# A 12-stage decoder kernel: masks of the turned scores moved from TensorE products to GpSimd selects, and another order at the end of a block step

## The reference

```python
# "block layer" (L1_attn): causal attention in windows of 128 that see the window before, norms and feed-forward
Q, K, V = (x @ proj + bias).reshape(B * 16, 256, 16)
sim = einsum('bnwd,bnkd->bnwk', qw * 16 ** -0.5, bk)       # keys: own and previous window
sim = where(key_position <= query_position, sim, -1e9)
attn = softmax(sim) @ bv
x = layernorm(x + attn, ln1_g, ln1_b)
ff = maximum(x @ ff1_w + ff1_b, 0.0) @ ff2_w + ff2_b
x = layernorm(x + ff, ln2_g, ln2_b)

# "cross-attention layer" (L1_xattn): a causal attention, then one over a context of 77 tokens
h = mha(x, x, x, causal=True)                              # 16 heads of 16
out = mha(h, encoder, encoder, causal=False)
```

## Time and profile before

| what | us |
|---|---|
| median of three runs | 3149.42 (3141.65 to 3149.58) |
| the profiled execution: span from first to last instruction | 3146.4 |
| its own time | not recorded apart from the span |
| TensorE, VectorE, ScalarE, GpSimd busy | 2939.7, 1864.8, 1253.5, 435.9 |
| block layer, 1137 to 1408: TensorE, VectorE, GpSimd busy | 242.29, 191.00, 21.48 |
| cross-attention layer, 1408 to 1688: TensorE, VectorE, GpSimd busy | 257.13, 191.32, 10.45 |

### The profile page before, as it was taken

The page is one execution under the profiler, slowest core; times in us unless marked ns, Lnnn a source line. Parts: engine busy times, 40 slices in busy tenths (PEclk is TensorE's granted clock), DMA queues, the critical chain, the costliest instruction groups (busy, mean ns, idle before and its releaser), DMA issues.

```text
span 3146.4 us, 52294 instructions
## 1 busy us (share of the span) xinstructions
PE 2939.7 (93%) x20677; PEld 1953.5 (62%) x20677; DVE 1864.8 (59%) x6449; ACT 1253.5 (40%) x1946; POOL 435.9 (14%) x458
## 2 busy tenths in 40 slices
PE   7999999998989889988998999899999999998998
PEld 4666666875555556655665566566666766766653
DVE  5534433599999636775777898574244344434455
ACT  2222221335656433323444678544323333323443
POOL 0010010114433221000000356300000000000000
PEclk9999999988999999999999899899999999998999
DMA  3000000010000100000000111100000000000000
GB/s 130 1 1 0 1 1 1 1 53 1 2 1 2 34 32 1 1 1 6 1 2 1 25 39 28 41 2 27 1 1 0 1 0 1 1 1 9 2 1 27
DMA packets 22028, 37.75 MB, mean 12 GB/s; under 512 B 2132, under 2 KB 19733, under 8 KB 20760
## 3 DMA queue, kind: packets, MB, share of 16 engines
q1 hardware_dynamic: 20968, 34.02, 3.2%
q10 hardware_dynamic: 816, 0.39, 0.1%
HBM read 26.81 MB, written 2.10 MB: 9 GB/s over the span
## 4 chain that ended last, share of the span: by engine, by line
PE 76%; DVE 17%; ACT 4%; issue 2%; DMA 0%; ACTq 0%; DVEq 0%; SPq 0%; POOL 0%; POOLq 0%
PE ps L416 44%; DVE arena L569 3%; PE ps L621 2%; PE ps L689 2%; PE ps L3098 2%; PE ps L3117 2%; ACT arena L675 2%; PE ps L1633 2%; PE ps L517 2%; PE ps L2353 2%; PE ps L2399 2%; DVE arena L1967 2%; PE ps L730 2%; PE ps L711 1%; PE ps L2971 1%
## 5 line engine op out<-in xcount | busy, mean ns | idle before, releaser
L416 PE MATMUL ps<-weights,arena 128*128 128x256 f32 (+4 forms) x2480 | 694.3, 429 | 41.3 <-DVE arena L1848 22.5
L416 PEld LDWEIGHTS ps<-weights,arena 128*128 128x128 f32 (+1 forms) x2480 | 459.5, 195 | 210.8 <-issue 92.9
L416 PE MATMUL ps<-arena,weights 128*128 128x256 f32 (+4 forms) x1726 | 558.9, 472 | 14.0 <-DMA weights<-in_w_L_attn 6.1
L416 PEld LDWEIGHTS ps<-arena,weights 128*128 128x128 f32 (+1 forms) x1726 | 315.1, 191 | 217.0 <-issue 156.5
L416 PE MATMUL ps<-arena 128*128 128x256 f32 (+4 forms) x1618 | 425.8, 416 | 6.8 <-ACT arena L4816 1.5
L416 PEld LDWEIGHTS ps<-arena 128*128 128x128 f32 (+2 forms) x1618 | 297.9, 188 | 115.4 <-issue 74.3
L569 DVE TENSOR_REDUCE arena<-ps 128x16 f32<-128x1232 f32 (+2 forms) x96 | 179.1, 1866 | 151.0 <-PE ps L547 51.8
L675 ACT ACTIVATE arena<-ps 77x2048 f32<-77x2048 f32 (+1 forms) x112 | 210.0, 1875 | 123.9 <-PE ps L621 61.8
L1967 DVE MATCH_REPLACE8 arena<-arena 128x77 f32<-128x77 f32 x1024 | 214.7, 228 | 0.0
L864 POOL TENSOR_TENSOR x<-x,weights 128x512 f32<-128x512 f32 x32 | 43.8, 1370 | 1194.9 <-DVE arena L830 1147.2
L2366 ACT ACTIVATE arena<-ps 128x1536 f32<-128x1536 f32 x128 | 185.5, 1451 | 51.4 <-PE ps L2355 44.6
(11 more groups left out here) (430 smaller groups left out, 4437.6 us busy)
## 6 DMA issues: line engine op xcount, KB each, us to landing
arena<-arena SPq DMA_DIRECT2D x156, 32.0 KB
weights<-in_w_L_ffn SPq DMA_DIRECT2D x1, 3848.0 KB, 11.5
weights<-in_w_L_attn SPq DMA_DIRECT2D x1, 3840.0 KB, 15.1
weights<-in_w_L_xattn SPq DMA_DIRECT2D x3, 1024.0 KB, 6.3
weights<-in_w_L_ffn SPq DMA_DIRECT2D x1, 3072.0 KB, 10.2
x<-in_x SPq DMA_DIRECT2D x2, 1024.0 KB
weights<-in_w_L_xattn SPq DMA_DIRECT2D x1, 2048.0 KB, 7.4
out<-x SPq DMA_DIRECT2D x8, 256.0 KB, 2.2
```

The costliest lines, as they stand in the source:

```text
L416: ins = k.nc.tensor.matmul(out, lhsT, rhs, start=start and i == 0, stop=i == n - 1)
```

## The change

Three edits, all for the causal batches of the two layers.

First, the "keyC" mask products of the turned scores go. Their job is done after the exponential, by GpSimd: `affine_select` keeps a probability where query >= key and writes 0.0 elsewhere. `hide_second_gpsimd` does `prob1` (four instructions of 128x4x128 behind `prob` 1), `hide_first_gpsimd` the first half of each 256 queries in `prob` (two behind `prob` 2, two behind `prob` 3); each signals `hidden`, and `pair_outputs_tensor` waits for `hidden` 2 + c. In round 0 two of the four places are now multiplied ahead of the turn of the maxima. Second, in the block layer the feed-forward's down product ("ff2") stands ahead of the next query, and the outputs of c = 0 come last; ScalarE's query copy stands ahead of `pair_raw_scalar` accordingly. Third, GpSimd's list is put in another order: its sum for x1 of batch n - 1 comes behind the selects of batch n, and in the cross-attention layer the bias sum of batch n + 1 comes behind the selects of batch n.

```diff
@@ turned_first_tensor
     after(pe, s, u, "top", u.a.rounds)
-    causal, places = u.a.causal, turned_places(u, 0)
-    if causal:
-        for i in range(4):
-            hide_later(k, k.ps[:, HI + i, :], mask_of(k, "keyC"))
-    else:
-        turned_products(k, s, u, places[0], True, False)
+    places = turned_places(u, 0)
+    ahead = 2 if u.a.causal else 1
+    for n, place in enumerate(places[:ahead]):
+        turned_products(k, s, u, place, n == 0, False)
     turn_tops_tensor(k, pe, s, u, b, at)
-    for place in places if causal else places[1:]:
+    for place in places[ahead:]:
         turned_products(k, s, u, place, False, False)
@@ turned_scores_tensor
     after(pe, s, u, "prob", r)
-    if u.a.causal:
-        for i in range(4):
-            hide_later(k, cut(k.ps[:, HI + i, :], slot=4)[:, 0::2, :], mask_of(k, "keyC")[:, 0:2 * P])
     for place in turned_places(u, r):
-        turned_maxima(k, s, u, place, not u.a.causal, False)
+        turned_maxima(k, s, u, place, True, False)
@@ pair_outputs_tensor
     if u.a.causal:
         after(pe, s, u, "kv")
+        after(pe, s, u, "hidden", 2 + c)
@@ new
+def hide_second_gpsimd(k, pool, s, u):
+
+    after(pool, s, u, "prob", 1)
+    for j in range(4):
+        prob = s.prob1[:, :, j * P:(j + 1) * P]
+        ins = k.nc.gpsimd.affine_select(prob, prob, [[0, 4], [1, P]], ALU.is_ge, 0.0, base=0, channel_multiplier=-1)
+    ins.then_inc(*s.sig.up(u.a.p + "hidden"))
+
+
+def hide_first_gpsimd(k, pool, s, u, c):
+
+    after(pool, s, u, "prob", 2 + c)
+    for j in (2 * c, 2 * c + 1):
+        prob = s.prob[:, :, j * SEQ:j * SEQ + P]
+        ins = k.nc.gpsimd.affine_select(prob, prob, [[0, 4], [1, P]], ALU.is_ge, 0.0, base=0, channel_multiplier=-1)
+    ins.then_inc(*s.sig.up(u.a.p + "hidden"))
@@ L1_xattn_gpsimd
-    for n in range(B):
-        bias_gpsimd(k, pool, s, n, "z", "bo2")
+    for u in s.steps:
+        if u.a.causal:
+            bias_gpsimd(k, pool, s, u.n, "z", "bo2")
+            hide_second_gpsimd(k, pool, s, u)
+            for c in (0, 1):
+                hide_first_gpsimd(k, pool, s, u, c)
@@ L1_attn_tensor
             turned_scores_tensor(k, pe, s, now, 2)
-            pair_outputs_tensor(k, pe, s, now, last, 0)
+        if older:
+            after(pe, s, older, "f", 2)
+            token_out_tensor(k, s, s.f, w_of(k, s.stage, "ff2", FF // P), 2, FF // P).then_inc(*s.sig.up("out_ps"))
         if soon:
             after(pe, s, soon, "kv")
             query_tensor(k, s, soon, s.zT, 3)
-        if older:
-            after(pe, s, older, "f", 2)
-            token_out_tensor(k, s, s.f, w_of(k, s.stage, "ff2", FF // P), 2, FF // P).then_inc(*s.sig.up("out_ps"))
+        if now:
+            pair_outputs_tensor(k, pe, s, now, last, 0)
@@ L1_attn_scalar
-            pair_raw_scalar(k, act, s, now, 0)
         if soon:
             query_scalar(k, act, s, soon, 3)
+        if now:
+            pair_raw_scalar(k, act, s, now, 0)
@@ L1_attn_gpsimd
         bias_gpsimd(k, pool, s, u.n, "z", "ln2_b")
-        pool.wait_ge(*s.sig.at("x1", 0, u.n, 1))
...
+        hide_second_gpsimd(k, pool, s, u)
+        for c in (0, 1):
+            hide_first_gpsimd(k, pool, s, u, c)
+        if u.n:
+            inner_bias_gpsimd(k, pool, s, s.steps[u.n - 1])
+    inner_bias_gpsimd(k, pool, s, s.steps[B - 1])
```

More of the change, by code:

```diff
@@ L103, in places @@
     return out, at
-COMMON = ("done", "dve_step", "z", "zT_ps", "zT", "qkv_ps", "q", "kv", "s_ps", "s_sb", "prob", "probT_ps", "probT_a",
+COMMON = ("done", "dve_step", "z", "zT_ps", "zT", "qkv_ps", "q", "kv", "s_ps", "prob", "hidden", "probT_ps", "probT_a",
           "probT_v", "o_ps", "raw", "back_ps", "o", "oT_ps", "oT", "out_ps", "ctx")
@@ L483, in narrow_signals @@
     if a.causal:
-        per.update(z=1, zT_ps=1, zT=1, k_ps=1, k=1)
+        per.update(z=1, zT_ps=1, zT=1, k_ps=1, k=1, hidden=3)
     return {a.p + name: n for name, n in per.items()}
@@ L2256, in L1_attn_vector, with inner_bias_gpsimd @@
             outer_sum_vector(k, dve, s, older, 2)
+def inner_bias_gpsimd(k, pool, s, u):
+    after(pool, s, u, "x1")
+    if u.n >= 2:
+        pool.wait_ge(*s.sig.at("sum", 0, u.n - 2, 1))
+    k.nc.gpsimd.tensor_tensor(s.x1b[u.n % 2], s.x1[u.n % 2],
+                              spread_of(k, s.stage, "ff2b").unsqueeze(1).broadcast_to([P, 2, D]), ALU.add)\
+        .then_inc(*s.sig.up("x1b"))
 def L1_attn_gpsimd(k, pool, s):
@@ L2262, in L1_attn_gpsimd @@
         bias_gpsimd(k, pool, s, u.n, "z", "ln2_b")
-        pool.wait_ge(*s.sig.at("x1", 0, u.n, 1))
-        if u.n >= 2:
-            pool.wait_ge(*s.sig.at("sum", 0, u.n - 2, 1))
-        k.nc.gpsimd.tensor_tensor(s.x1b[u.n % 2], s.x1[u.n % 2],
-                                  spread_of(k, s.stage, "ff2b").unsqueeze(1).broadcast_to([P, 2, D]), ALU.add)\
-            .then_inc(*s.sig.up("x1b"))
+        hide_second_gpsimd(k, pool, s, u)
[4 more added lines that the diff above has]
+    inner_bias_gpsimd(k, pool, s, s.steps[B - 1])
 GROUPS = NH1 // 4
```

## The result

The changed kernel took 3156.51 us (median of 11 executions, 3150.93 to 3161.72) beside 3144.96 us for the kernel before (11 executions, 3135.09 to 3149.58): ratio 1.0034, 95% interval 1.0022 to 1.0047, so slower by 0.34%, where 3148.0 and no measurable change were forecast. (The forecast was added to a median of three executions, 3149.42, which lay 4.5 us above the 3144.96 of all eleven; as a difference it was -1.4 us, and +11.6 was measured.) Measured four times in all (experiments 9, 13 and 14), the ratio was 1.0034, 1.0012, 1.0033 and 1.0029; the median of the 46 executions is 3152.7 us. The profiled execution of after has a span of 3156.2 us.

What follows compares the result with a forecast made beforehand. VectorE was taken to end the block steps of batches 3 to 5, with 0.71 us to spare. Block layer + 4.5 and cross-attention - 5.9 gave - 1.4 us on span 3146.4, plus 3.0 to the median: 3148.0, range 3135 to 3161.

Steps and rivals of the forecast that it cites:

- TensorE's side: Per batch step: fewer masks on the chain shorten TensorE's part by 0.4 + 0.54 + 0.54 = 1.5 us.
- rival 4: Outputs on TensorE: it waits for selects of 1.15 us each; + 7 us, 3156, chance 0.13.
- The lock: Block steps of batches 3 to 5: six selects each hold a VectorE operation 0.41 us, 2.45 us a step.
- Rivals 1 and 3: VectorE: 1, lock hardly bites, about 3134, chance 0.24; 3, each select costs the whole 0.64 us, about 3165, chance 0.12.
- The other block steps: Block layer: batch 0 - 2.3 us, batch 1 0, batch 2 - 1.3, batch 6 + 0.3, batch 7 + 2.6.
- The cross-attention layer: All its batches together: shorter TensorE rounds, less what waits for selects give back, - 5.9 us.
- The 0.65: Ahead of cross steps: outputs of c=1 wait for two selects, so 0.75 us is given back.
- The sum is + 4.5 - 5.9 = - 1.4 us on the profiled execution: Whole kernel: block layer + 4.5 us and cross-attention layer - 5.9, on a span of 3146.4 us.

Runs made afterwards that it cites:

- experiment 9: The changed kernel measured again, unchanged, against the kernel before: 3146.24 us, ratio 1.0012.
- 13: The changed kernel measured a third time, unchanged, against the kernel before: 3156.49 us, ratio 1.0033.
- 14: The changed kernel measured a fourth time, unchanged, in the same call as the third, against the kernel before: ratio 1.0029.
- experiment 2: The change in the block layer alone, cross-attention layer as in the kernel before: 3150.87 us, ratio 1.0025 to the kernel before.
- Experiment 15: Repeat of the changed kernel without the GpSimd selects and the waits for them: 3129.28 us, ratio 0.9953 to the kernel before.
- 1: The changed kernel without the GpSimd selects and the waits for them, half of the masking left out: 3129.73 us, ratio 0.9947 to the kernel before.
- 3: The change in the cross-attention layer alone, block layer as in the kernel before: 3145.91 us, ratio 1.0003 to the kernel before.
- 5: The kernel before with the block layer's new order alone: 3139.59 us, ratio 0.9985 to the kernel before.
- 6: The changed kernel with the first round masked by TensorE again, four selects per batch instead of eight: 3140.24 us, ratio 0.9979 to the kernel before.
- 7: The changed kernel plus two unread 512-column TensorE products per block step from batch 3 on: 3150.03 us, ratio 1.0016 to the kernel before.
- 10: The kernel before plus two unread 512-column TensorE products per block step from batch 3 on: 3151.29 us, ratio 1.0021 to the kernel before.
- 11: The changed kernel plus two unread 512-column TensorE products at each of two block-step places, the second in all steps: 3150.67 us, ratio 1.0017 to the kernel before.
- 12: The changed kernel with half the selects and, in cross steps, the next norm turned ahead of c=1's outputs: 3136.48 us, ratio 0.9972 to the kernel before.
- 8: The changed kernel with four selects of 128x512 joined into one of 128x2048: 3151.82 us, ratio 1.0030 to the kernel before.

## Why the prediction was wrong

**TensorE's side, right in the block layer.** 0.44 us for L592 to L630 (1.20 to 0.76; forecast 0.4) and 0.55 twice (forecast 0.54). TensorE waits for no select there, so rival 4 is out, although its number, 3156, is the one first measured: that is chance.

**The lock, right in kind, too dear.** The prediction had six operations held at 0.41 us, 2.45 us a step. Measured are five at 0.38 (2.72 us instead of 0.81 in the rows above, 1.91), and 1.84 by leaving the selects out. Two of the five (L2072 and L277) have one tensor as input, so it wasn't two operands in SBUF, as the prediction had it, that picked them. The step of batches 3 to 5 is 30.70 us: 29.59, less the 0.71 to spare, plus 1.83. Forecast were 31.3. Rivals 1 and 3 (28.9 and 34 us) are out.

**The other block steps**, from experiment 9, whose clock fell least: batch 0 -1.9 us (forecast -2.3), batch 2 -1.5 (-1.3), batch 6 -0.5 (+0.3), batch 1 -1.8 (0; before's step has 3.4 us more at 1.2 GHz, so part of this is clock). Batch 7's step with what drains behind it is 4.0 longer (+2.6), with 10.2 us at 1.2 GHz against 3.4; at 6.8 in experiment 2 it is 0.9 longer. Together the block layer was put at +4.5 us, and is -1.6 in experiment 2, whose block layer has before's 13.7 us at 1.2 GHz.

**The cross-attention layer, too hopeful.** Forecast was -0.8 for batches 2 and 3 and -0.3 for 4 to 6; measured are -0.34, -0.31 and -0.07 to +0.12, and -0.46 for batch 7 (forecast -0.8): -1.1 us in all where -3.3 were forecast. Experiment 15 splits this: without selects the pairs of batches 2, 3 and 4 to 6 are 0.98, 0.98 and 1.35 us shorter than before, where the prediction had 1.5 for TensorE's side, and the selects give back 0.64, 0.67 and 1.3. The 0.65 was forecast as 0.75.

Why the masks are worth 1.0 and not 1.5 can be read in batch 2. Counted from its first maximum, the exponentials start at 13.82, 17.81 and 21.63 us before, and at 13.37, 17.37 and 20.64 in experiment 15. The first gains its 0.45, but the second gains no more than that. TensorE's turn of the means waits for VectorE now (L728, the mean) and starts as late as before, and the projections behind it keep TensorE until the second round:

```profile
1464.12 0.66 PE L735 MATMUL ps<-ident,arena 128*128 128x128 f32 x4 [0.39 <-DVE arena L728]
1464.61 1.89 PE L416 MATMUL ps<-arena,weights 128*128 128x256 f32 x8
1466.43 0.29 PE L630 MATMUL ps<-arena,pick 32*128 32x256 bf16 x4
```

That is 16.02 us behind the first maximum, where before's second round began at 15.94. So the first round's 0.45 is lost in this wait, and what is left is the second round's start without its mask (0.45) and the third's (0.54).

Batches 0 and 1 in after had 6.8 us more at 1.2 GHz each than before, so these two terms can't be read.

**The step that failed** is "The sum is + 4.5 - 5.9 = - 1.4 us on the profiled execution". Every term in it was a duration at before's clock. The changed kernel has TensorE at 1.2 GHz for some 33 us more of an execution, worth 11 to 13 us by the slopes; no term and no rival held that. What the sum did cover came out at -2 to -4.5 by that estimate, so -1.4 was about right, by errors that cancel: the block layer was put 6 us too dear, the cross-attention layer too hopeful. In the profiled executions the block layer is 11.5 us longer, with 27 more us at 1.2 GHz in it, and all the rest 1.7 us shorter.

**What brings the clock down.** In a full-clock step like that of batch 5 TensorE was idle for 0.63 us before, 0.64 with the order alone, 1.38 without selects, 1.63 with half, 1.08 or 0.2 with products added; in none of these ten profiles (before, 1, 3, 5, 6, 7, 10, 11, 12, 15) did a step of batches 4 to 6 fall. It was idle for 2.3 us with both masks and 3.0 in the changed form (first, 2, 8, 9, 13, 14), and in five of these seven steps did fall. So in these steps it goes with the idleness that the held VectorE chain makes; it isn't certain in an execution: experiments 2 and 9 are without it.

But these steps hold only 10.2 of the 27 us that the block layer of after has more. Batch 0's 13.7 us stand in experiments 3, 5, 6 and 12 as well, in 3 with before's block layer, so the profile can't lay them to the change. And over the executions the selects don't explain all: 155 us with the order alone, 173 and 176 with the masks gone as well and no select, 195 with everything, 187 with the selects and all the masks. So taking the mask products off TensorE goes with some 20 us more at 1.2 GHz, without any select.

Of the 23 to 27 us that the selects cost, an estimate finds some 20: 6.5 in the block steps of batches 3 to 6, 5.7 in the pairs of batches 2 to 6 and batch 7, and 7 to 8 for 20 us more at 1.2 GHz. That added products bring the time back by this way alone isn't shown: they cost time as well, and a measurement of the same kernel moved by up to 10 us. What makes one measurement of the changed kernel differ from another stays open.

A kernel with GpSimd's selects but without TensorE's wait for them wasn't tried, since the masked values are the ones that TensorE reads.

## What to carry to other kernels

Before a term is booked as gain, ask which engine ends the step then: here 1.5 us taken from TensorE could bring 0.71 at most, and the GpSimd work that paid for it cost VectorE's chain 1.83 through the lock. The new order, with only the masks that stand on TensorE's path moved (half the selects) and the one wait that they make covered, was worth 0.28% (the order alone 0.15%). Moving all of the masks lost 0.1 to 0.3%. A change that makes TensorE idle in a step should be priced at both clock levels, and a difference below half a per cent asks for the same kernel measured more than once, with the granted clock beside each time.

## What the hardware showed that was not expected

A select of 128x512 took 0.60 to 0.66 us in the block layer and one of 128x2048 took 2.00; a held VectorE operation of two columns took 0.49 to 0.59 us beside the first and 1.37 beside the second, instead of 0.16. Two stretches of the same code, 277.4 and 267.5 us, differed in the granted clock (0.93 and 0.97), while the busy times of VectorE and ScalarE were the same within 0.3 us. In one measurement of four the changed kernel's executions had 16 to 22 us less at 1.2 GHz than in the others, while the kernel before stayed at 161 to 162 us in four measurements on three chips.
